# Turning the raw blocks ahead of the sums' emptying, and projecting a pair in two parts

## The reference

```
# L0 attention, per pair of channels: 16 channels of rank 64, so 8 pairs
u = x @ U.T * s ; v = x @ V.T * s            # per channel [T, 64]
q = sigmoid(u @ v.T)                         # [T, T]
g = (q @ v) @ U + (q.T @ u) @ V              # summed over channels, times s
# L0 ffn: router, top-k of 64 tokens for each of 8 experts, attention of each
logits = sigmoid(x @ Wr.T); topk; QKV; rope; softmax; @ Wo; scatter-add
# L1 attention (structured, a running sum over time) and L1 ffn (gate, up, down)
```

## Time and profile before

| | |
|---|---|
| median of 3 runs | 1463.75 us (1462.65 to 1465.48) |
| profiled execution: time, span | 1468.4 us, 1466.6 us |
| PE busy | 1389.9 us, 95% |
| DVE busy | 903.6 us, 62% |
| ACT busy | 688.9 us, 47% |
| POOL busy | 44.1 us, 3% |
| mean granted TensorE clock | 0.982 |
| DMA | 51.37 MB, 35 GB/s |

### The profile page before, as it was taken

One profiled execution on the slowest core, in us unless ns is written; L12 is line 12 of the kernel. 1 busy time (PEld: TensorE's weight loads), 2 busy tenths in 40 slices (PEclk: granted clock), 3 DMA queues, 4 the chain that ended last, 5 costly groups with the idle time before them and its releaser, 6 DMA issues.

```text
span 1466.6 us, 24503 instructions
## 1 busy us (share of the span) xinstructions
PE 1389.9 (95%) x7806; PEld 793.9 (54%) x7806; DVE 903.6 (62%) x1559; ACT 688.9 (47%) x1058; POOL 44.1 (3%) x41
## 2 busy tenths in 40 slices
PE   6999798899998999999999999999999999999968
PEld 3566444455564555555565555555655555555534
DVE  8868443366655665656655656556555666566657
ACT  3556344444443544454444543454544454454421
POOL 4000400000000000000000000000000000000000
PEclk9999899999999999999999999999999999999988
DMA  6012222112221212221112211221212111221110
GB/s 207 1 31 66 43 35 31 26 29 35 30 30 31 33 27 30 36 32 31 26 26 39 36 29 24 36 34 28 30 29 36 32 26 27 38 30 27 25 30 8
DMA packets 302620, 51.37 MB, mean 35 GB/s; under 512 B 280545, under 2 KB 300769, under 8 KB 302465
## 3 DMA queue, kind: packets, MB, share of 16 engines
q1 hardware_dynamic: 302128, 47.82, 19.4%
q0 software_dynamic: 336, 1.64, 0.3%
HBM read 11.64 MB, written 4.19 MB: 11 GB/s over the span
## 4 chain that ended last, share of the span: by engine, by line
issue 85%; DVE 1%; PE 1%; POOL 1%; ACT 0%; POOLq 0%; DVEq 0%
PE psum L1231 1%; DVE arena L917 0%; DVE arena L923 0%; DVE arena L915 0%; POOL u_w_hl L608 0%; POOL v_w_hl L608 0%; POOL rstd_s L623 0%; POOL up_hl L608 0%; DVE arena L939 0%; PE psum L1575 0%; DVE xn_s L663 0%; POOL u_w_hl L605 0%; POOL v_w_hl L605 0%; DVE x_all L932 0%; POOL up_hl L605 0%
## 5 line engine op out<-in xcount | busy, mean ns | idle before, releaser
L1172 ACT ACTIVATE arena<-psum 128x1024 f32<-128x1024 f32 x504 | 476.0, 1030 | 636.5 <-PE psum L1231 636.3
L1231 PE MATMUL psum<-arena 128*64 128x512 f32 x2016 | 466.0, 605 | 26.0 <-DMA arena<-blocks 14.6
L1231 PEld LDWEIGHTS psum<-arena 128*64 128x64 f32 x2016 | 135.0, 138 | 290.0 <-issue 244.7
L1231 PE MATMUL psum<-u_parts,v_parts 64*128 64x512 f32 x1536 | 199.5, 404 | 11.9 <-issue 11.2
L1231 PE MATMUL psum<-v_parts,u_parts 64*128 64x512 f32 (+1 forms) x1568 | 201.9, 397 | 0.0
L866 DVE TENSOR_SCALAR o_hl<-psum,sums 128x512 fp32r<-128x512 f32 x126 | 94.4, 749 | 162.1 <-PE psum L1231 162.1
L1231 PEld LDWEIGHTS psum<-u_parts,v_parts 64*128 64x128 f32 x1536 | 141.7, 187 | 93.1 <-issue 45.3
L1231 PEld LDWEIGHTS psum<-v_parts,u_parts 64*128 64x128 f32 (+1 forms) x1568 | 145.3, 184 | 81.5 <-issue 51.1
L868 DVE SCALAR_TENSOR_TENSOR o_hl<-psum,sums,o_hl 128x512 fp32r<-128x512 f32 x126 | 94.6, 751 | 4.5
L1121 ACT ACTIVATE arena<-psum 128x512 f32<-128x512 f32 x128 | 77.1, 625 | 18.5 <-PE psum L1231 18.5
L923 DVE TENSOR_TENSOR arena<-psum,arena 128x512 f32<-128x512 f32 x96 | 64.6, 689 | 33.7 <-PE psum L1231 31.7
(11 more groups left out here) (211 smaller groups left out, 1517.0 us busy)
## 6 DMA issues: line engine op xcount, KB each, us to landing
arena<-blocks SPq DMA_DIRECT2D x1008, 32.0 KB, 2.0
x_all<-in_x SPq DMA_DIRECT2D x4, 512.0 KB, 5.4
upper<-in_we SPq DMA_DIRECT2D x8, 256.0 KB, 2.7
expert_rows<-upper SPq DMA_DIRECT2D x16, 128.0 KB, 2.5
xn_s<-expert_rows SPq DMA_DIRECT2D x8, 256.0 KB, 2.9
out<-x_all SPq DMA_DIRECT2D x8, 256.0 KB, 2.5
arena<-in_e POOLq DMA_DIRECT2D x1, 896.0 KB, 5.7
arena<-in_wi POOLq DMA_DIRECT2D x1, 576.0 KB, 5.7
```

The source lines that it names most:

```text
L1172: nc.scalar.activation(th_of(un), psum[:, at:at + 2], ACT.Tanh, scale=0.5 * FACTOR_SCALE ** 2).then_inc(s_th, 2)
L1231: return nc.tensor.matmul(out, lhsT, rhs, start=start, stop=stop)
```

## The change

1. **Turn before emptying.** In even halves DVE's `turn` moves from after `evac_o` (and `add_y`) to directly ahead of it.
2. **Projection in two parts.** `pj` becomes `pj0` (three matmuls on sum o = 0 of the same pair, in the odd half) and `pj1` (three on sum o = 1, in the next even half). Each has a bank and an `add_g` of its own. Nothing changes in the number of matmuls; DVE has one more `add_g` for each pair.
3. **Gate and up of the first chunk** go from half 5 to half 3.
4. **First tokens by TensorE.** The `turn` and the 16 DMAs of batch 0's pair 1 are gone. PE transposes `u_raw` and `v_raw` (4 transposes each, `prep` with k = 3 and 4) between steps of the last expert, and ACT copies the two banks into `tok`.
5. **PE's loop** runs batch 1 written out and then three passes of two batches each. The loops of DVE, ACT and SP keep one batch a pass.
6. **Start.** ACT normalises the odd batches (`odd_rows`, Identity with scale and bias), DVE the even ones. The logits of two batches go into 32 output rows each, at rows 0 and 64 of the bank.

```diff
-PREP_IN_HALF = [("pu", "pv", "pj"), ()]
+PREP_IN_HALF = [("pu", "pv", "pj1"), ("pj0",)]
...
-FULL_STEPS = {1: [("back", 0)], 2: [("norm", 0)], 3: [("kq", 0), ("v", 0)], 12: [("down", 0)], 15: [("yo", 0), ("yo", 1)]}
-FULL_STEPS |= {h: [("gate", f), ("up", f)] for h, f in ((5, 0), (6, 1), (9, 2))}
+FULL_STEPS = {1: [("back", 0)], 2: [("norm", 0)], 3: [("kq", 0), ("v", 0), ("gate", 0), ("up", 0)], 12: [("down", 0)], 15: [("yo", 0), ("yo", 1)]}
+FULL_STEPS |= {h: [("gate", f), ("up", f)] for h, f in ((6, 1), (9, 2))}
...
             def part_rows(h):
                 dve.wait_ge(s_rstd, h + 1)
-                for n in range(h * X_PART, (h + 1) * X_PART):
-                    if n >= 2:
-                        dve.wait_ge(s_xT, n - 1)
-                    normalised(xn_g[:, n % 2], n, mv1[:, n, :, 0:1], rstd1[:, n].unsqueeze(2)).then_inc(s_xn, 1)
+                odd, even = h * X_PART + 1, h * X_PART
+                nc.vector.scalar_tensor_tensor(shift1[:, odd], mv1[:, odd, :, 0], -1.0, rstd1[:, odd], ALU.mult, ALU.mult)\
+                  .then_inc(s_shift, 1)
+                if h:
+                    dve.wait_ge(s_xT, even - 1)
+                normalised(xn_g[:, 0], even, mv1[:, even, :, 0:1], rstd1[:, even].unsqueeze(2)).then_inc(s_xn, 1)
...
             prep_v(0, 1)
-            dve.wait_ge(s_prep_w, 1)
-            turn(0, 0, first_blocks)
             expert_rows(E - 1, 1, E // 2 - 1)
...
+                    if o == 0:
+                        if not some_before:
+                            for n in range(2):
+                                dve.wait_ge(s_ymv[n], 16 * E)
+                        turn(i, j)
                     evac_o(g, j, o, some_before)
                     for r in range(ROUNDS):
                         if second and Y_AT[r] == h:
                             add_y(r, i - 1)
-                    if o == 0:
-                        if not some_before:
-                            for n in range(2):
-                                dve.wait_ge(s_ymv[n], 16 * E)
-                        turn(i, j, later_blocks)
...
+            def odd_rows(n):
+                act.wait_ge(s_shift, n // 2 + 1)
+                if n >= 2:
+                    act.wait_ge(s_xT, n - 1)
+                for k in range(TB):
+                    ins = nc.scalar.activation(xn_g[:, 1, k], x_all[:, n, k], ACT.Identity, bias=shift1[:, n, k:k + 1],
+                                               scale=rstd1[:, n, k:k + 1])
+                ins.then_inc(s_xna, 1)
...
+            def prep_tok(k, w, bk):
+                act.wait_ge(s_prep_full, prep_index(0, k) + 1)
+                copy(tok[:, 1, w].rearrange("p k c -> p (k c)"), bk[:]).then_inc(s_prep_free, 1)
...
+            def logits(pair):
+                pe.wait_ge(s_xnT, 2 * pair + 2)
+                for g in range(2):
+                    ins = mm(bank[2][g * 64:g * 64 + 32], wr_b[:, pair * 32:pair * 32 + 32], xn1T[:, 2 * pair + g],
+                             pair == 0, pair == B // 2 - 1)
+                return ins
...
-            def project(g, j, bk):
-
-                pe.wait_ge(s_oe, g * 2)
-                was = (j - 1) % PAIRS
-                passes = [(o, a, b) for o in range(2) for a, b in ((0, 0), (0, 1), (1, 0))]
-                for n, (o, a, b) in enumerate(passes):
-                    ins = mm(bk[:], w_hl[o][:, a, was * D:(was + 1) * D], o_hl[:, o, b], n == 0, n == len(passes) - 1)
+            def project(kind, g, j, bk):
+
+                o, of = (0, j) if kind == "pj0" else (1, (j - 1) % PAIRS)
+                pe.wait_ge(s_oe, g * 2 + 1 if kind == "pj0" else g * 2)
+                for n, (a, b) in enumerate(((0, 0), (0, 1), (1, 0))):
+                    ins = mm(bk[:], w_hl[o][:, a, of * D:(of + 1) * D], o_hl[:, o, b], n == 0, n == 2)
                 ins.then_inc(s_pj_full, 1)
...
             iteration(0, True, False)
-            with pe.Fori(1, B) as i:
-                iteration(i, True, True)
+            iteration(1, True, True)
+            with pe.Fori(1, B // 2) as m:
+                for n in range(2):
+                    iteration(m * 2 + n, True, True)
             iteration(B, False, True)
```

More of the change, by code:

```diff
@@ L160, in first_middle_of @@
 def first_middle_of(h):
-    work = [w for w in MIDDLE[h] if w[0] in ("pu", "pv", "pj") and w != ("pj", 1)]
+    work = [w for w in MIDDLE[h] if w[0] in ("pu", "pv", "pj0", "pj1") and w != ("pj1", 1)]
     return work + [("sc", 0)] * (h == FIRST_SCATTER_HALF)
@@ L197, in is_prep, with projected_count, moved_count @@
 def is_prep(work):
-    return work[0] in ("pu", "pv", "pj", "sc")
+    return work[0] in ("pu", "pv", "pj0", "pj1", "sc")
 def prep_index(g, k):
-    return g * 2 + 3 + k
+    return 3 + k if is_first(g) else g * 2 + 5 + k
+def projected_count(kind, g):
+    return g * 2 if kind == "pj0" else g * 2 - 1
+def moved_count(i, j):
+    return (i + (j > 0)) * MOVED
 def is_first(g):
@@ L231, in scatter_bank @@
         def scatter_bank(i):
-            return x_bank(("sc", 0), not isinstance(i, int))
+            return x_bank(("sc", 0), not (isinstance(i, int) and i == 0))
         x_all = sb("x_all", [P, B, TB, D])
@@ L550, in _, with move_tokens @@
             load_rows(0)
+            def move_tokens(i, j):
+                sp.wait_ge(s_turned, i * PAIRS + j)
+                for r in range(QUARTERS):
+                    for a in range(QUARTERS):
+                        sp.dma_start(tok[32 * r:32 * r + 32, (j + 1) % 2, :, :, 32 * a:32 * a + 32].rearrange("t w k c -> t (w k) c"),
+                                     blocks[32 * a:32 * a + 32].rearrange("t w (k r c) -> t (w k) r c", k=TB, r=QUARTERS)[:, :, r])\
+                          .then_inc(s_moved[j], 16)
             for j in range(1, PAIRS):
-                move_tokens(0, j, later_blocks)
+                move_tokens(0, j)
                 if j == 2:
@@ L855, in add_g @@
                     before = gT[:]
-                if isinstance(i, int) and i == 0 and j == 3:
+                if isinstance(i, int) and i == 0 and (kind, j) == ("pj1", 3):
                     dve.wait_ge(s_scf, 1)
+                if not (isinstance(i, int) and i == 0) and (kind, j) == ("pj0", 0):
+                    dve.wait_ge(s_scf, i + 1)
                 nc.vector.scalar_tensor_tensor(gT[:], bk[:], 0.5 * FACTOR_SCALE ** 2, before, ALU.mult, ALU.add).then_inc(s_pj_free, 1)
@@ L992, in iteration @@
                             prep_v(g, (j + 1) % 2)
-                        elif work[0] == "pj":
-                            add_g(i, j)
+                        elif work[0] in ("pj0", "pj1"):
+                            add_g(i, j, work[0])
                         elif not is_prep(work) and second:
@@ L1032, in transposed @@
                 copy(xn1T[:, n], bank[par][:]).then_inc(s_xnT, 1)
-            pairs(fori_of(act), transposed)
+            def odd_rows(n):
[6 more added lines that the diff above has]
+                ins.then_inc(s_xna, 1)
+            odd_rows(1)
+            for n in range(0, B, 2):
+                transposed(n, 0)
+                transposed(n + 1, 1)
+                if n + 3 < B:
+                    odd_rows(n + 3)
             act.wait_ge(s_lg, 1)
-            nc.scalar.activation(tk_work, bank[2][0:E * B], ACT.Exp, scale=-1.0).then_inc(s_ex, 1)
+            for g in range(2):
+                ins = nc.scalar.activation(tk_work[g * 32:g * 32 + 32], bank[2][g * 64:g * 64 + 32], ACT.Exp, scale=-1.0)
+            ins.then_inc(s_ex, 1)
             act.wait_ge(s_first, 16 * len(first_consts))
@@ L1233, in _, with transposes @@
             pe.wait_ge(s_first, 16 * len(first_consts))
-            def transposes(n, par):
-                pe.wait_ge(s_xn, n + 1)
-                if later(n):
+            def transposes(n):
+                par = n % 2
+                if par == 0:
+                    pe.wait_ge(s_xn, n // 2 + 1)
+                else:
+                    pe.wait_ge(s_xna, n // 2 + 1)
+                if n >= 2:
                     pe.wait_ge(s_xnT, n - 1)
```

126 lines of the change are left out of this document (67 added, 59 removed).

## The result

The changed kernel takes **1453.42 us** (median of 5 runs, 1453.11 to 1455.29), the kernel before in the same comparison 1464.23 (5 runs, 1462.65 to 1468.57). The ratio is 0.9926, 95% interval 0.9910 to 0.9941: 10.8 us faster, where 21.3 were forecast. The profiled execution of the change is its median (1453.42 us, span 1451.6), while that of before lay 4.2 us above its own; the two spans differ by 15.0 us.

What follows compares the result with a forecast made beforehand. TensorE, busy 95% of the span, was taken as the bound, so only its waits or slow work could be gained. 33.9 us gained less 12.6 lost gave 21.3 net: 1463.75 to 1442.4 us, range 1431 to 1457.

Steps and rivals of the forecast that it cites:

- Baseline: Whole kernel: the median lies 4.65 us below the profiled time, and the same difference was applied to the forecast.
- Start: Up to the top-k: ACT's share of normalising and paired logits bring the top-k earlier, 3.1 us gained.
- First tokens by PE: Experts to half 4 of batch 0: the 5.45 us wait goes, the emptying comes just in time, 5.4 us gained.
- the clock: PE near 154 to 158 us: transposes fill short waits before the low clock; 1.0 us taken as gained.
- Batch 0: Pairs of batch 0: 16.43 us instead of 18.16, moves hidden; with half 0 of batch 1, 13.0 us gained.
- Where the loop begins: Six loop starts: DVE's chain, not PE, sets half 1's fourth unit after 11.5 us; 7.3 us gained.
- Rival C: Where the loop begins: PE's four lost jumps are worth their waits in full, 7.3 us, so 1435 us; chance 0.08.
- Inside batches 1 to 7: Short token waits go, 2.1 us gained; 11.2 us lost to a late emptying, 1.4 to the added add_g.
- the waits in half 8: Inside batches 1 to 7: five short waits for moves, 2.1 of the 14.6 us, go.
- The stall in half 5: Batches 1 to 7: PE waits 1.6 us for DVE's late emptying of half 4, seven times, 11.2 us lost.
- the other even halves: Batches 1 to 7: DVE idle time or PE's y_round covers the turn, cost nothing; uncovered, up to 1.2 us each.
- Tail: After the last emptying: three matmuls instead of six, 0.7 us, and gate and up fill DVE's idle, 1.3; together 2.0.

Runs made afterwards that it cites:

- holding POOL: The change, with POOL's split of the second weight and of gate and up held until DVE's splits of half 2 of batch 0 are done: 1448.61 us, ratio 0.9889.
- the turn's run: The kernel before, with only the turn moved ahead of the emptying in every even half: 1453.23 us, ratio 0.9918.
- one part: The change, with the projection in one part of six matmuls in the even half in batches 1 to 7, two parts only in batch 0: 1441.20 us, ratio 0.9843.

## Why the prediction was off

Direction, range and most places were right; the size was not: 10.8 us instead of 21.3. The step that failed is a term that the sum has at nothing: moving half of the projection to an odd half was put as an even exchange, 0.75 us there for 0.75 us here, and in halves 7, 11 and 13 it costs 0.2 us more than it saves. 5.2 us went missing in the stretch where that stands, the largest piece. The rest are the profile's distance from the median, carried over (4.2), the first tokens (2.4) and the start (1.5), less what the other stretches gave above their terms. Point by point:

- *Baseline.* "I apply the same difference to it": 4.65 us between profiled time and median were taken over to the change. Its profiled execution is its median, so 4.2 us of the forecast gain (by the median of five runs, 1464.23) are only this.
- *Start*, 3.1 forecast, 1.6 in the trace. Top-k began at 27.57, 27.92 and 27.86 us in three profiles of the old start and at 25.08 to 26.85 in the eleven of the new. What the sum left out stands in the change's trace: PE waits 0.57 us for ACT's last four tiles (1.64 us for four, where DVE takes 1.1), and ACT takes the exponential in two operations, 1.19 us in place of 0.59.
- *First tokens by PE*, 5.4 and 1.0 for the clock. Transposes and copies cost nothing, and the wait went, as forecast. But I took the splits beside POOL as they stood, where the four took 4.9 us, and they got worse: 5.9 us, for what needs 2.5 alone. So PE waits 3.51 us for the emptying that was to come just in time, and the clock falls as it did behind the old wait. The low clock of 154 us, for which I took 1.0 us gained, was worth nothing: the wait for the blocks hid it. 4.0 us came of 6.4; holding POOL gives the rest and more.
- *Batch 0*: right. A pair is 16.43 us to the hundredth, the stretch gave 14.2 against 13.0. In the turn's run a pair is 17.07 us; so 1.09 of the 1.73 are the turn's and 0.64 the two parts'.
- *Where the loop begins*: right in sum (7.2 of 7.3) and in what sets the change's time: DVE's chain, 11.4 us in the mean against 11.5. But what paid was the turn. Alone, with every jump of PE kept, it brings the chain to 11.8 us and these halves from 131.1 to 121.4, less than the change's 123.9. Rival C fell with PE's old loop (no slower) and DVE's unrolled one (6.0 us less). By the Trainium skill's Runtime: NRT & Kernel Launch, Instruction fetch mechanics, a taken branch whose target lies outside the loaded window stalls; both engines' rows agree in so far as each waits on issue where it jumps (1.2 to 2.2 us on PE with its old loop, 2.4 to 2.6 on DVE) and DVE doesn't where it is written out; what it waits for they don't show. And only the later of two engines that jump at the same place pays.
- *Inside batches 1 to 7*, the step that failed: I counted `pj0` in an odd half as the 0.75 us that the even half loses. It costs 0.90 to 0.97 in halves 7, 11 and 13, where it stands alone between other shapes, and the even halves lose 0.7: 0.2 in each of 21 halves for one more change of shape, 4 to 5 us of the 5.2 missing here. The terms beside it were off by about 1 us each. Halves 3 and 5 grew by 11.7 us beyond their two `pj0`, where the stall was put at 11.2 (its waits are 10.0); half 2 got 0.55 us shorter in place of 0.75; and the waits in half 8 were six of 2.9 us, not five of 2.1, and gave 3.2. The Trainium skill has the rule, TensorEngine Tiling (Array Packing), Key Properties: "Mode switching requires drain". I did not weigh it. The stall in half 5 was right (1.43 of 1.6), the other even halves at nothing too.
- *What the parts were worth.* I summed one list and did not ask which edit paid for which term. The turn alone is worth the whole result (ratio 0.9918 against 0.9926). The two parts of the projection cost 12.2 us in batches 1 to 7, for a gain of some 4 in batch 0 (0.64 a pair) and perhaps the tail's. The start and the first tokens gave some of it back, by the stretches of the trace (1.6 and 4.0 us); neither was tried alone, nor gate and up in half 3. PE's loop is worth nothing that these runs can tell.
- *Tail*: 3.8 against 2.0. From the weighted sums of half 15 to the end it is 58.2 us before and 58.0 with the turn alone, 54.4 in the change and 55.1 with one part; so some 3 us seem to come with gate and up in half 3 and under 1 from the two parts, which isn't shown: the same tail varies between profiles, from 54.4 to 56.0 us in those of the change and its near kin.

## What to carry to other kernels

Order on an engine that two others wait for trades one wait for another: price both ends, and at the speed that the other edits give the waiting engine, not at that of the old trace. Evening out two half cycles is worth it only where the shorter one really waits (batch 0 here); elsewhere it splits a block of like matmuls and brings the busy engine sooner to whoever was just in time. And test a bundle part by part: here one line carried all of it, one edit cost 12 us, and two causes outside the change, POOL beside DVE and DVE's own jump, were worth 11 together (11.5 when both were added to one part in a single kernel). A wait can also be worth more than its length, where matmuls run slow behind it.

## What the runs showed of the hardware

- One more change of shape in PE's stream (64 rows, 128 rows, 64 columns) costs 0.20 to 0.22 us: with `pj0` alone in a half, and again with `pj0` ahead of the rows. Where it stands beside gate and up it adds none (half 9: 10.39 us with it, 9.70 without, three matmuls' time).
- DVE's operations with two inputs in SBUF wait for POOL's: 2.74 us against 0.69, and its copy from SBUF took 1.61 against 0.43 to 0.66, beside POOL operations of 2.4 us. The block transpose (1.23 and 1.24) and the emptying's first operation, from PSUM (0.70, and 0.71 with POOL held back), don't. The Trainium skill's SBUF — State Buffer, Who interferes with whom, has the rule: a DVE instruction with two SBUF inputs contends with a GpSimd instruction that reads SBUF, casts can contend in the two-port modes, where one engine holds a shared port pair for a whole instruction, and one SBUF input outside these modes doesn't contend. Trace and page agree.
- PE's granted clock fell to 0.50 at the wait of 3.51 to 3.53 us in all seven profiles that have it, in it or within 1 us behind it, and stayed at 1.00 behind one of 3.10, with the same matmuls on either side. The 16 weighted matmuls that follow took 4.45 to 5.05 us in the seven, against 3.65.
